# First loads in another order, and the modulation of later batches copied later

## What is computed

```python
scale, shift = split(cond @ W_emb + b_emb)            # cond: 8 x 1024, W_emb: 1024 x 2048
xn  = rms_norm(x) * g_norm * (1 + scale) + shift       # per batch
q, k, v = heads(xn @ W_qkv)                           # 16 heads of 64
o   = softmax(rms_norm(q) @ rms_norm(k).T / 8) @ v
out = x + o + o @ W_out
```

## Time and profile before

| | us |
|---|---|
| timed runs | 2233.69, 2234.15, 2225.84; median 2233.69 |
| the profiled execution | 2237.3 |
| its span, first to last instruction | 2235.5 |
| PE busy | 2132.8 (95%) |
| DVE busy | 1702.2 (76%) |
| ACT busy | 1524.8 (68%) |
| POOL busy | 1039.3 (46%) |
| mean granted TensorE clock | 0.982 of full |

### The profile page before, as it was taken

How to read it: one execution, slowest core, us unless ns; L and a number is a source line. 1 busy time by engine, 2 the same in 40 slices (tenths; PEclk the granted TensorE clock), 3 DMA queues, 4 the chain that set the end, 5 groups by cost and what they waited for, 6 DMA issues and landing times.

```text
span 2235.5 us, 36400 instructions
## 1 busy us (share of the span) xinstructions
PE 2132.8 (95%) x11880; PEld 1884.2 (84%) x11880; DVE 1702.2 (76%) x3043; ACT 1524.8 (68%) x3261; POOL 1039.3 (46%) x1325
## 2 busy tenths in 40 slices
PE   7899865999999999999999999999999999999999
PEld 3778755799988998789987999889998899979998
DVE  4899975768875888758877688757887588775785
ACT  4688874567864788547875578647886488755773
POOL 3876754533653345623445335443356234563330
PEclk9999986999999999999999999999999999999999
DMA  8676587785668756685667856677567866678663
GB/s 316 249 283 254 194 316 290 291 326 205 213 222 315 266 213 215 249 325 202 238 208 289 324 203 221 226 291 278 204 212 272 318 220 232 206 274 295 217 208 104
DMA packets 128108, 558.17 MB, mean 250 GB/s; under 512 B 13488, under 2 KB 31920, under 8 KB 114352
## 3 DMA queue, kind: packets, MB, share of 16 engines
q1 hardware_dynamic: 127920, 555.84, 68.7%
HBM read 478.20 MB, written 77.59 MB: 249 GB/s over the span
## 4 chain that ended last, share of the span: by engine, by line
PE 80%; DMA 7%; DVE 4%; ACT 4%; issue 2%; POOL 2%; SPq 0%; ACTq 0%; DVEq 0%; POOLq 0%
PE proj_bank L687 17%; PE proj_bank L689 16%; PE proj_bank L688 16%; PE flip_bank L817 8%; PE score_bank L808 5%; PE pv_bank L828 5%; PE score_bank L809 4%; PE pv_bank L829 4%; DMA w_ring<-wo_store 3%; DMA w_ring<-qkv_store 2%; PE score_bank L781 2%; PE flip_bank L788 1%; ACT probs L995 1%; DVE pt_lo L1300 1%; DVE neg_max L1289 1%
## 5 line engine op out<-in xcount | busy, mean ns | idle before, releaser
L687 PE MATMUL proj_bank<-w_ring,xa_hi 128*128 128x384 f32 x1792 | 631.5, 352 | 16.1 <-DMA w_ring<-qkv_store 4.6
L689 PE MATMUL proj_bank<-w_ring,xa_lo 128*128 128x384 f32 x1792 | 607.7, 339 | 0.0
L688 PE MATMUL proj_bank<-w_ring,xa_hi 128*128 128x384 f32 x1792 | 606.5, 338 | 0.0
L1300 DVE TENSOR_TENSOR pt_lo<-flip_bank,pt_hi 128x512 fp32r<-128x512 f32 x512 | 348.1, 685 | 109.6 <-ACT pt_hi L1005 104.4
L995 ACT ACTIVATE probs<-score_bank,neg_max 128x512 f32<-128x512 f32 x512 | 352.6, 691 | 114.7 <-DVE neg_max L1289 110.1
L1005 ACT CAST pt_hi<-flip_bank 128x512 fp32r<-128x512 f32 x512 | 296.5, 587 | 178.7 <-PE flip_bank L817 97.4
L1289 DVE TENSOR_REDUCE neg_max<-score_bank 128x1 f32<-128x512 f32 x512 | 346.8, 685 | 56.1 <-PE score_bank L809 53.8
L687 PEld LDWEIGHTS proj_bank<-w_ring,xa_hi 128*128 128x128 f32 x1792 | 340.3, 190 | 40.6 <-DMA w_ring<-qkv_store 8.1
L688 PEld LDWEIGHTS proj_bank<-w_ring,xa_hi 128*128 128x128 f32 x1792 | 340.9, 190 | 13.5
L689 PEld LDWEIGHTS proj_bank<-w_ring,xa_lo 128*128 128x128 f32 x1792 | 339.4, 189 | 0.0
L817 PE MATMUL flip_bank<-ident,probs 128*128 128x128 f32 x2048 | 304.5, 274 | 23.4 <-DVE pt_lo L1300 9.7
(11 more groups left out here) (107 smaller groups left out, 3854.8 us busy)
## 6 DMA issues: line engine op xcount, KB each, us to landing
w_ring<-qkv_store SPq DMA_DIRECT2D x392, 768.0 KB, 5.6
w_ring<-wo_store SPq DMA_DIRECT2D x98, 1024.0 KB, 4.9
qkv_store<-w_ring SPq DMA_DIRECT2D x56, 768.0 KB, 4.1
x_tile<-in_x SPq DMA_DIRECT2D x36, 512.0 KB, 7.0
wo_store<-o_lo SPq DMA_DIRECT2D x32, 512.0 KB, 3.5
w_raw<-in_x SPq DMA_DIRECT2D x56, 256.0 KB, 5.4
out<-w_raw SPq DMA_DIRECT2D x56, 256.0 KB, 6.8
w_raw<-in_w_qkv SPq DMA_DIRECT2D x16, 768.0 KB, 9.3
```

The source lines that it names most:

```text
L687: nc.tensor.matmul(dst, a_hi, w[:, 0, :], start=start, stop=False, skip_group_check=shared)
L688: nc.tensor.matmul(dst, a_hi, w[:, 1, :], start=False, stop=False, skip_group_check=shared)
L689: return nc.tensor.matmul(dst, a_lo, w[:, 0, :], start=False, stop=stop, skip_group_check=shared)
L1300: nc.vector.tensor_tensor(pt_lo[n % 2][:, :], flip_bank[u % 2][:, :], f32(pt_hi[n % 2][:, :]), ALU.subtract).then_inc(flip_freed["VectorE" ...
```

## The change

The loads that SyncE issues ahead of its list are put into another order: the conditioning first, then the first six tiles of W_emb with q0 behind the second and q1 behind the fourth, the four constants, q2, tile 6, x0, tile 7, x1, q3, x2, x3. The waits of each load stay with it. `save_mod` is called after VectorE's step X6 of batch 0 instead of after X0.

```diff
-                        if is_first(b + d) and n == 0:
+                        if is_first(b + d) and n == 6:
                             save_mod()
@@
-            for kt in range(KT):
+
+            def load_emb(kt):
                 slot, uses = emb_slot(kt)
                 if uses > 1:
                     sp.wait_ge(emb_used, slot + 1)
                 sp.dma_start(emb_tile[slot], emb_rows[kt]).then_inc(emb_loaded[slot], 16)
-                if kt == 0:
-                    sp.dma_start(cond_sb[:, :, :], cond_t).then_inc(cond_loaded, 16)
-                if kt == NEMB - 1:
-                    for q in range(2):
-                        load_raw(("C", 0, 0), q)
-            for r in range(TT):
-                load_x(0, r)
+
+            sp.dma_start(cond_sb[:, :, :], cond_t).then_inc(cond_loaded, 16)
+            for kt in range(6):
+                load_emb(kt)
+                if kt in (1, 3):
+                    load_raw(("C", 0, 0), kt // 2)
             for dst, src in nc_const:
                 sp.dma_start(dst, src).then_inc(const_loaded, 16)
-            for q in range(2, 4):
-                load_raw(("C", 0, 0), q)
+            load_raw(("C", 0, 0), 2)
+            for kt in (6, 7):
+                load_emb(kt)
+                load_x(0, kt - 6)
+            load_raw(("C", 0, 0), 3)
+            for r in (2, 3):
+                load_x(0, r)
```

## The result

| | before | changed |
|---|---|---|
| median of 20 runs each | 2232.96 us (2225.84 to 2241.37) | 2236.19 us (2232.55 to 2243.07) |
| ratio, 95% interval | | 1.0021 (1.0012 to 1.0031) |
| span of the first profiled execution | 2235.5 us | 2232.5 us |

The changed kernel is 0.21% slower by the ratio, 4.7 us of 2233, between 2.7 and 6.9; the two medians of the table lie 3.2 us apart, inside that interval. Its one profiled execution is 3.0 us *shorter* than that of before. Single executions of one kernel differ by 10 to 16 us here, so the profile tells where the time stands, and the ratio tells how much it is.

The account below looks back on a forecast made before the run. Bound first by load bytes and modulation matmuls, from about 37 us by VectorE's nearly gapless list. Terms 4.9 - 1.9 + 1.4 - 0.2 = +4.2 us on 2233.7 gave 2237.9 us, range 2229 to 2246.

Parts of the forecast that it names:

- part 3: Load queue behind q2's wait: x3 lands late, so ScalarE's copies of the modulation rows start +4.9 us (4.5 to 5.5).
- part 4: `save_mod` on VectorE's list: -1.9 us at the old place, +1.4 us (0.8 to 1.9) behind X6.
- Parts 1 and 2: First loads: conditioning first costs 0 to +0.4 us, covered; q0 and q1 between tiles bring no stall and no gain.
- Part 5: VectorE's sums beside GpSimd's: their overlap shrinks by 0.3 us, -0.2 us (0 to -1.3).
- A: The x loads stay hidden and the copies start when the matmuls end: +0.3 us, 2234.0; chance 0.08.
- D: The load queue does not keep the order of issue, so landings and time stay, 2233.7; chance 0.02.
- B: SyncE's blocked issues delay one another, x3 at 40, `save_mod` at full price: +7.1 us, 2240.8; chance 0.14.
- C: TensorE's first products run at half clock longer; 100 more such matmuls give 2252.9 us; chance 0.06.

## Why the prediction was right

**By the number.** Forecast were +4.2 us on before, 2237.9, within 2229 to 2246, and no change beyond 0.5% with 0.91. Measured are 2236.19 and +4.7 us (2.7 to 6.9). The sign and the root of the loss, the late x tiles, were the forecast ones. That the sum hit so close is in part luck. The head was forecast to be 2.8 us late (first product at 47.8) and was 4.45 us late (49.48): part 3 was too small, and most of the gain of part 4 did not come. What made the sum good again is the +1.4 us for `save_mod` at its new place, which no run shows.

**Parts 1 and 2: right, but for 0.1 us.** TensorE's first matmul of the modulation started at 6.69 instead of 6.18 (forecast 0 to +0.4; 6.61 and 6.50 in the other two profiles). Its tiles stalled it 0.28 and 0.17 us, both for tiles 6 and 7. Both were covered by the x tiles. With the x tiles ahead nothing of these parts can be told from zero, 1.0004 (0.9994 to 1.0014).

**Part 3: right in kind, 1.2 us too small.** The term was +4.9 (4.5 to 5.5), measured +6.05. The term mis-sized is the gap of the DMA: I took 0.4 us of a possible 1.0, and it was 1.7. The wait of q2 ended 0.6 us later than 21.5, because the matmuls had started later, and the queue moved 0.68 MB too little. The landing of x3 at 39.1 lies beyond the end of my range for it (38.5).

**Part 3, what hangs on it: incomplete.** I named ScalarE's copies as the one way by which x3 binds. The changed kernel's own profile shows another that ended last: VectorE scales x3 ahead of `mod_now`, and was ready for it 0.8 us after Z0. The run with the modulation rows first shows a third, by x2 and VectorE's list; with the first two taken away the first product moved by 0.07 us. ScalarE's order alone was not changed in any run; after these readings no gain is to be expected of it.

**Part 4: right in kind, the gain too large.** The two modulate steps stand back to back, as forecast. But the 1.9 us were read from the one profile of before in which `save_mod` stood beside GpSimd's sums; it is 0.7 us in the three others and 1.5 in the run with the loads alone. With the old loads 0.4 us reached the first product, since the sums then run beside GpSimd's. The price at the new place, 1.4 us in the forecast, can't be read: `save_mod` took 1.4 us there (58.07 to 59.45). The net of -0.5 us lies within what the run with `save_mod` alone allows (-2.5 to +2.5).

**Part 5: mis-sized, twice.** I moved the overlap with GpSimd's sums by 0.3 us and left it at the sums. In truth it stretched the scaling of x3 and two small steps (+1.1), and then spared the sums and Y0 (-1.2). The scaling took 1.47 us beside GpSimd's sums and 0.75 without them. The small steps of 0.90 and 0.70 us end at 43.52 and 44.47, and GpSimd's sums beside them at 43.49 and 44.44. The Trainium skill, in SBUF — State Buffer, calls the shared port an exclusive lock: these ends agree with it, as does a gain at the sums of 1.2 us, of the size of one whole wait. The net of the whole part is near nothing, as in my 0.2 us, because what one instruction was spared another paid.

**The carrying.** First product against ratio, in the order of the marks: 44.65, 1.0000; 45.23, 1.0004; 49.41, 1.0018; 49.48, 1.0021; 51.12, 1.0021; 51.30, 1.0027. A head late by 4.4 to 6.3 us ends 4 to 6 us late. The forecast that the delay lasts to the end holds, to within the 2 us that the intervals leave. That it is VectorE's list that passes it on is shown for the head only.

**Rivals.** A and D did not come: x3 landed at 39.1, in order of issue. B's time, +7.1 us, is just outside the interval; its dry queue was real, its blocked issues were not (q2 to x1 took 0.38 to 0.68 us each). C did not come. The clock of the changed kernel, as the earlier trace rows:

```profile
40.00:50.00 10.00, 6.59 (x34) 5.37 (x35) 9.04 (x19) 5.57 (x15) 6.88 (x8) 0.52 0.57 238
50.00:60.00 10.00, 7.44 (x42) 6.57 (x41) 9.80 (x20) 9.96 (x25) 5.18 (x4) 0.97 0.21 82
60.00:320.00 260.00, 233.66 (x1263) 203.19 (x1262) 239.41 (x412) 208.74 (x459) 188.39 (x216) 0.97 0.67 252
```

From 40 to 50 us 0.52 against 0.50, and 0.97 against 0.99 from 60 us on. From 50 to 60 us it is 0.97 against 0.84, which does not belong to the change: the other profiles of both kernels have 0.80 to 0.83. The half level (1.2 GHz) stands in much of the stretch from 40 to 50 us in both kernels, a little more in the changed one: its other profiles have 0.50 and 0.52, those of before 0.66. No run shows a price of it.

## What to carry to other kernels

Moving loads costs what the last of them is needed for: the bytes are the same, so ask which tile is now last, and what stands behind its consumers on every engine's list. A load that must wait for a buffer holds all loads behind it on its queue; put what needs no wait ahead of it. Before an order is mended at one engine, look for the second chain of the same length. And before a term is read from one profile, read it in a second: here a gain of 1.9 us was 0.7 in three others.

## What had not been expected

- Moving instructions out of a list can give back little although they stood on the path: of the 0.7 to 1.9 us of `save_mod`, 0.4 reached the first product, as its neighbours moved under GpSimd's sums (Y0 1.48 instead of 0.68 us).
- A head that starts 1.2 us later can deliver at the same time: in three of four profiles of before the first modulate step came at 38.7 to 38.8 instead of 37.45, and the first product at 45.0 all the same.
- Taking GpSimd's sums away from VectorE's scaling (0.75 instead of 1.47 us) did not move the first product (9.36 against 9.34 us behind the copies).
- Profiles of one kernel differ in the waits for the same stored weights by 1.2 to 10.3 us. A single profile of each kernel would have shown the slower one as the faster.
